# A fused FFN, delta-rule and FFN kernel on one core: where the second norm and the key pieces stand in the eight steps of a block

## What is computed

```
x = x + 0.5 * ffn(layernorm(x))      # recurrent over the batch index b = 0..7
x = x +       attn(layernorm(x))     # recurrent over the 1024 tokens
x = x + 0.5 * ffn(layernorm(x))

ffn, step b:  f = sigmoid(x_b Wf + c Uf + bf);  i = sigmoid(x_b Wi + c Ui + bi)
              g = tanh(x_b Wc + c Uc + bc);     c = f * c + i * g
     result:  tanh(x_b Wo + c_final Uo + bo)
attn:         s = x W^T;  k = rmsnorm of each head (16 heads of 16) of x
              per token, head: S = lam*S; S += beta * k (v - k^T S); o = k^T S, v = -s
              result: layernorm(s + o)
```

## Time and profile before

| | |
|---|---|
| median of three runs | 1555.78 us |
| profiled execution | 1562.62 us, its span 1560.8 us |
| TensorE matmul, weight load | busy 1380.0 us (88%), 1277.7 us (82%) |
| VectorE, ScalarE, GpSimd | 924.6 us (59%), 689.2 us (44%), 197.3 us (13%) |
| chain that ended last | TensorE 61%, VectorE 21%, issue 9%, ScalarE 7% |
| mean granted TensorE clock | 0.94 |
| period 4 (stage alone) | 96.5 us, TensorE busy 87.7 |
| period 8 (joined stage) | 145.5 us, TensorE busy 126.6 |
| period 12 (no pieces left) | 82.2 us, TensorE busy 78.6 |

### The profile page before, as it was taken

The page is one execution under the profiler, slowest core; times in us unless marked ns, Lnnn a source line. Parts: engine busy times, 40 slices in busy tenths (PEclk is TensorE's granted clock), DMA queues, the critical chain, the costliest instruction groups (busy, mean ns, idle before and its releaser), DMA issues.

```text
span 1560.8 us, 61982 instructions
## 1 busy us (share of the span) xinstructions
PE 1380.0 (88%) x27811; PEld 1277.7 (82%) x27811; DVE 924.6 (59%) x2208; ACT 689.2 (44%) x1585; POOL 197.3 (13%) x230
## 2 busy tenths in 40 slices
PE   4889899998989899888888988889899999999887
PEld 4878798888979788777877887878788989898776
DVE  2646686777867766558655774664444645554532
ACT  2253454545445444443444444344445445444332
POOL 0001010010100100002400320040130404040400
PEclk9999999998999989998889979989999999999999
DMA  4011112112211323232224222421534333332000
GB/s 128 1 41 68 42 44 84 58 75 67 78 63 58 124 64 95 91 119 65 73 82 131 68 90 64 158 70 47 166 88 119 98 110 107 90 122 80 28 28 28
DMA packets 64201, 125.39 MB, mean 80 GB/s; under 512 B 12352, under 2 KB 33088, under 8 KB 61888
## 3 DMA queue, kind: packets, MB, share of 16 engines
q1 hardware_dynamic: 63936, 121.43, 24.3%
HBM read 62.13 MB, written 59.24 MB: 78 GB/s over the span
## 4 chain that ended last, share of the span: by engine, by line
PE 61%; DVE 21%; issue 9%; ACT 7%; DVEq 0%; ACTq 0%
PE ps L426 29%; PE ps L493 7%; PE ps L1007 6%; PE ps L818 4%; PE ps L642 4%; PE ps L991 4%; DVE ln_bn L83 3%; ACT gates L443 3%; PE ps L667 2%; ACT ffn_rows L101 2%; DVE ig L469 2%; PE ps L386 1%; ACT gates L450 1%; PE ps L478 1%; DVE prod L743 1%
## 5 line engine op out<-in xcount | busy, mean ns | idle before, releaser
L426 PE MATMUL ps<-cst,wt 128*128 128x128 f32 x2688 | 360.7, 290 | 8.3 <-DVE cst L471 7.8
L426 PEld LDWEIGHTS ps<-cst,wt 128*128 128x128 f32 x2688 | 331.3, 201 | 20.0 <-DVE cst L471 9.1
L426 PE MATMUL ps<-ffn_rows,wt 128*128 128x128 f32 x2304 | 300.3, 288 | 17.4 <-DVE hs L506 6.4
L426 PEld LDWEIGHTS ps<-ffn_rows,wt 128*128 128x128 f32 x2304 | 285.7, 203 | 25.9 <-issue 15.8
L465 DVE TENSOR_TENSOR fc<-gates,cst 128x256 f32<-128x256 f32 x112 | 51.7, 461 | 285.0 <-ACT gates L443 284.9
L443 ACT ACTIVATE gates<-ps,colv 128x128 f32<-128x128 f32 x448 | 127.1, 365 | 173.9 <-PE ps L426 173.6
L1007 PE MATMUL ps<-e,kgb 32*128 32x64 f32 x4032 | 129.6, 275 | 7.9 <-issue 4.1
L1007 PEld LDWEIGHTS ps<-e,kgb 32*128 32x128 f32 x4032 | 120.6, 189 | 16.6 <-issue 10.6
L1096 POOL TENSOR_TENSOR ffn_rows<-ffn_rows,rowv 128x256 f32<-128x256 f32 x64 | 54.3, 882 | 573.5 <-DMA ffn_rows<-x_scratch 573.5
L818 PE MATMUL ps<-inv_cols,kv 32*32 32x32 f32 x8192 | 92.4, 201 | 34.3 <-DVE zbd L1037 17.4
L618 POOL TENSOR_TENSOR kg_rows<-key_rows,g_tok 128x512 f32<-128x512 f32 x32 | 46.4, 1478 | 594.9 <-DVE key_rows L581 594.9
(11 more groups left out here) (117 smaller groups left out, 1793.5 us busy)
## 6 DMA issues: line engine op xcount, KB each, us to landing
kg_scratch<-kg_rows SPq DMA_DIRECT2D x32, 512.0 KB, 3.9
xs_scratch<-xs_out SPq DMA_DIRECT2D x32, 512.0 KB, 3.6
xsb<-xs_scratch SPq DMA_DIRECT2D x64, 256.0 KB, 3.5
kgb<-kg_scratch SPq DMA_DIRECT2D x256, 64.0 KB, 2.6
ffn_rows<-x SPq DMA_DIRECT2D x32, 256.0 KB, 3.4
x_scratch<-ffn_rows SPq DMA_DIRECT2D x32, 256.0 KB, 2.7
e_scratch<-e SPq DMA_DIRECT2D x256, 32.0 KB, 1.7
ffn_rows<-e_scratch SPq DMA_DIRECT2D x8, 1024.0 KB, 6.2
```

Source lines behind the costliest of these rows:

```text
L426: mm = pe.matmul(banks[g][:, col:col + P], wt[:, w, k, m * P:(m + 1) * P], rhs, start=(x in (0, FI)), stop=(k == KT - 1 and (t == 0 or x > ...
```

## The change

The table `PERIOD` is rewritten, and two pieces are cut in two. ln2 keeps the statistics, and the coefficients become lc2. apply becomes apa and apb, four rows each. gt0 goes from the first list of step 1 to the second of step 0, ahead of the statistics. lc2 and apa stand in step 1 behind gt1; inv1 and apb in step 2's first list; lt0 in its second; lt1, v01, v23, tt0 and tt1 follow half a step later each than before, as do ta0 to ta2. ln1 goes from the end of step 5 to its first list, lc1 to the first of step 6, ap0 to the second of step 6 and ap1 to the first of step 7. The square waits for the whole apply by a semaphore, on the engine that does the apply itself.

```diff
-PERIOD = {0: ([(2, "g3")], [(1, "ln2")]),
-          1: ([(3, "ta4"), (2, "gt0")], [(2, "gt1"), (3, "ta5"), (2, "inv1"), (1, "apply")]),
-          2: ([(1, "lt0"), (3, "ta6")], [(1, "lt1"), (2, "al"), (1, "square"), (2, "inv2")]),
-          3: ([(3, "ta7"), (1, "v01")], [(1, "v23"), (2, "inv3"), (1, "sums")]),
-          4: ([(2, "tt0")], [(2, "tt1"), (1, "rms"), (1, "key")]),
-          5: ([(2, "ta0")], [(1, "keys"), (2, "ta1"), (-1, "ln1")]),
-          6: ([(1, "kt0"), (2, "ta2")], [(1, "kt1"), (1, "km0"), (-1, "lc1")]),
-          7: ([(1, "g0"), (-1, "ap0")], [(1, "g1"), (1, "km1"), (-1, "ap1")])}
+PERIOD = {0: ([(2, "g3")], [(2, "gt0"), (1, "ln2")]),
+          1: ([(3, "ta4")], [(2, "gt1"), (1, "lc2"), (3, "ta5"), (1, "apa")]),
+          2: ([(2, "inv1"), (3, "ta6"), (1, "apb")], [(1, "lt0"), (2, "al"), (1, "square"), (2, "inv2")]),
+          3: ([(1, "lt1"), (3, "ta7")], [(1, "v01"), (1, "sums"), (2, "inv3")]),
+          4: ([(1, "v23")], [(2, "tt0"), (1, "rms"), (1, "key")]),
+          5: ([(2, "tt1"), (-1, "ln1")], [(1, "keys"), (2, "ta0")]),
+          6: ([(1, "kt0"), (2, "ta1"), (-1, "lc1")], [(1, "kt1"), (2, "ta2"), (1, "km0"), (-1, "ap0")]),
+          7: ([(1, "g0"), (-1, "ap1")], [(1, "g1"), (1, "km1")])}
...
             if name == "ln2":
                 dve.wait_ge(ff.x_done, 4 * (n + 1))
                 ln2.stats_bn(dve, n, xt[b.p], bn_buf[0])
+            elif name == "lc2":
                 ln2.coefficients_bn(dve, n, bn_buf[0])
...
-            if name == "apply":
+            if name in ("apa", "apb"):
                 if n > 0:
                     filled(act, "gt", n - 1, 3)
-                ln2.apply(act, n, xn2, xt[b.p], range(8))
+                ln2.apply(act, n, xn2, xt[b.p], range(4) if name == "apa" else range(4, 8))
...
             elif name == "square":
+                act.wait_ge(ln2.applied, 8 * (n + 1))
                 act.activation(key_half, key_rows, ACT.Square).then_inc(sq_done, 1)
```

## The result

The changed kernel takes 1633.31 us (median of 4, 1629.45 to 1635.51), the kernel before on the same chip 1559.35 (4 runs, 1555.32 to 1564.24): ratio **1.047**, 95% interval 1.0426 to 1.0514. It is 74 us slower where 45 were forecast, and above the forecast's high end of 1625. A repeat beside other runs gave 1634.34 us, ratio 1.0504 (1.0452 to 1.0557).

A forecast was written before the change was run, and what follows sets the result against it. It took TensorE's queue to bound the kernel, lengthened by waits at its head and the half clock behind them. The alone stage's 31.9 us plus the joined stage's 13 made 45 us, so 1601 us, range 1557 to 1625.

The forecast's parts named there:

- alone stage: Periods 0 to 5, without the state hops: new costs 59.6 us against old 27.7 in periods 2 to 5, net +31.9.
- old gt wait: Step 1, periods 2 to 5: TensorE's wait for gt0's banks goes, 15.1 us, with 10.4 of half clock behind it.
- joined stage: Periods 6 to 9, where the state hops run beside the step: +3.6 us for each of 6 to 8, +13 together.
- term (c): Joined stage, step 3: inv1 now lies ahead of VectorE's z copy, for which TensorE stands: +3.6 us.
- Term (b): Joined stage: ScalarE's copy of e now stands behind half an apply that awaits gt1's eviction and the coefficients: +2.1 us on the hop.
- Term (a): Joined stage: gt0 waits for its Gram eviction: +0.5 us.
- term (d): Joined stage: v23 leaves step 3 and lt1 enters: -2.6 us.
- Step 4 gets v23 and loses one inverse copy: even: Joined stage, step 4: the values piece that enters and the copy that leaves cancel, so no cost.
- The port question: Step 5: L469 gets back 0.85 us beside GpSimd, sum unchanged; tt1's copy 1.6 us later only at the upper end.
- Faster: Rival: al in step 2 and ta0 do not wait, only the removed wait counts: -22 us, 1534; chance 0.13.
- No change: Rival: the waits come but the clock stays high and the joined stage absorbs its own: +11 us, 1567; chance 0.11.
- One wait only: Rival: al's bank is free in time, ta0's wait stays with its half clock: +17 us, 1572; chance 0.12.

The follow-up runs named there:

- e1: The new table in periods 0 to 5 alone, the old order from period 6 on: 1597.66 us, ratio 1.0264 to the kernel before.
- e4: The changed kernel with al put ahead of lt0 in step 2: 1635.34 us, ratio 1.0518 to the kernel before.
- e5: The changed kernel with tt0 and tt1 put back where they stood in step 4: 1606.90 us, ratio 1.0299 to the kernel before.
- e9: The kernel before, in periods 0 to 5 alone, with only gt0 moved to step 0 behind the third Gram part: 1543.27 us, ratio 0.9909.
- e6: The changed kernel with inv1 put back at the end of step 1: 1616.28 us, ratio 1.0384 to the kernel before.
- s3: The kernel before, from period 6 alone, with only inv1 moved from step 1 to the head of step 2: 1570.09 us, ratio 1.0076.
- s2: The kernel before, from period 6 alone, with the norm pieces, gt0, lt and the values moved as in the change: 1571.96 us, ratio 1.0097.
- e11: The changed kernel with the values v01 and v23 put back in step 3: 1640.65 us, ratio 1.0527 to the kernel before.
- s1: The kernel before, from period 6 alone, with the solve pieces tt0 to ta2 moved later as in the change: 1576.20 us, ratio 1.011.
- e10: The kernel before, in periods 0 to 5 alone, with only the norm's coefficients moved behind gt0 in step 1: 1543.38 us, ratio 0.9902.
- e3: The changed kernel with the unit ta1 moved back from step 6 to behind ta0 in step 5: 1633.65 us, ratio 1.0492 to the kernel before.

## Why the forecast was wrong, and where it was right

**The alone stage: right in its waits.** In period 4 gt0 waits 1.50 us (forecast 1.5), al 3.88 (4.5), ta0 4.10 (3.7); cst of step 5 comes 13.1 us after that of step 4 (14). Behind gt0 and al the X takes 4.47 us, behind ta0 4.57, not 5.5; the forecast had put slower matmuls behind two of these waits and none behind gt0. In period 2 al waits only 2.07 us, but lt0 ahead of it waits 3.66 for the apply, for which the forecast had no term. The sum was +31.9 against +32.3 in the profile, of which TensorE's idle made 24 (waits forecast: 21.5) and its busy time 9 (half clock forecast: 10.4); the repeat has +35.9, e1 +36.7. e4 and e5 confirm the queues by moving them. But the match is partly luck, two errors that cancel. I priced the old gt wait and its half clock at 25.5 us and the gt0 wait that replaces it at 6, a gain of 19.5. e9, which does only that, gained 13.6 in periods 1 to 5. So the removal was over-priced by 6. All the rest was forecast at 31.9 + 19.5 = 51.4 and measured 32.3 + 13.6 = 45.9, over-priced by about as much.

**inv1: right.** In the alone stage undoing it changed nothing beyond the scatter (e6); in the joined stage term (c), 3.6 us in each of three periods, 10.8 in all, is what s3 lengthened periods 6 to 9 by: 10.8. The wait and its size are right; that they agree to the tenth is luck, given a scatter of some 6 us between traces. TensorE's waits grew by more (14.8).

**The copy of e, al and lt: one sized right, one too low, two not priced.** Term (b), +2.1 per hop, was 6.3 for three; the hop's update waits 5.4 us longer in s2. Term (a), 1.5 for three, is gt's wait: 3.3 us where there was none. Not on the list were al, which waits for ScalarE in the joined stage too (+4.0), and lt (+3.0). And term (d), -2.6 for each of three periods, was work moved and counted as gain: in s2 the step without v23 got 10.8 us shorter over the four periods, and the step with it 10.3 longer. e11 says the same from the other side. Forecast for the part 0, measured +11.0, or +15 by its runs.

**The solve pieces: the step that failed.** The record says "Step 4 gets v23 and loses one inverse copy: even", and has no line at all for ta0, ta1 and ta2 in the joined stage. s1 measures this: +22.2 us in periods 6 to 9 of its profiled execution, +16 by the medians, either way the largest of the three parts and near half of the stage's loss. tt1's bank must wait for the z copy of the hop, which VectorE does behind the rms chain and the key product: 9.5 us in s1, and 5.9 more than gt and tt waited before; the changed kernel shows it in period 8:

```profile
968.73 2.29 DVE L582 TENSOR_TENSOR key_rows<-key_rows,rms 128x2048 f32<-128x2048 f32 x1
...
971.27 1.39 DVE L1039 COPY zbd<-ps 16x512 f32<-16x512 f32 x2
...
972.80 1.14 PE L804 MATMUL ps<-ident,inv 128*128 128x128 f32 x8 [3.71 <-DVE zbd L1039]
```

That is the rule of the code that `refill` waits in this stage for the state copies of the last hop. I had used it for ta in step 3 and not for the piece that newly stands first in a step. Another 6.6 is idle without a semaphore (the last section says what comes with it), and what is left, 9.7, is slower matmuls: TensorE's busy time in these periods rose by 9.6 us (477.4 to 487.0), and the half-clock length by 30.8 us, or 44 against the other kernels with the old order. The forecast priced half clock in the joined stage at zero, except for the upper end.

So 13 forecast was 10.8 (c), about 0 for the norm pieces and the solve pieces, +2 for period 9; measured apart by the traces, 10.8, 11.0 and 22.2. Two terms were at or near nothing without a reason that held: the solve pieces, and v23's move, a gain of 7.8 that did not exist. In the changed kernel the two late parts also meet, as lt1 waits 7.66 and 5.03 us in periods 7 and 8 for the z copy behind inv1, here in period 8 (12.7 in all; 4.1 in e6, 3.0 in s2, none in s3); in exchange ta waits less. Its total, 39.9, is below the sum of the parts, 44.0, by no more than the traces scatter.

```profile
935.04 1.39 DVE L1039 COPY zbd<-ps 16x512 f32<-16x512 f32 x2
...
936.58 1.94 PE L633 MATMUL ps<-ident,key_rows 128*128 128x128 f32 x8 [5.03 <-DVE zbd L1039]
```

**The port question.** The copy L756 from PSUM beside GpSimd's products took 1.98 us, no longer than elsewhere (2.04 at 426.74 in the same period), L469 took 0.42 us where it had 1.28, and GpSimd's four products 4.10 where they had 6.57. L469 says nothing by itself here, since it starts at 439.02 and GpSimd had ended at 438.60; but in e5, where it again stands beside GpSimd's products, it took 1.27. The upper end's term of 1.6 us a period did not come. This is as the Trainium skill has it ("SBUF — State Buffer", Who interferes with whom): a VectorE operation with two inputs in SBUF contends with a GpSimd operation that reads SBUF, one with at most one such input, outside the two-port modes, does not. The change of place was worth about 0.85 us on a product behind another wait, and did not show in the time.

**The rivals.** Faster (1534) fell with al's wait of 3.88 us; its gain was real but belonged to one edit: e9 and e10 have it at 1543, without the pieces that follow. The Trainium skill ("Perfetto Trace Analysis", Optimizing Scalar/DVE Operations) says that breaking up instructions may let work end sooner where ScalarE or VectorE cause bubbles elsewhere. No run here splits a single instruction, so none tests this by the letter. For groups of instructions both outcomes are on record: e10, where the coefficients were cut off and put behind an eviction, gained 1%; the change put the cut apply and the eviction of ta6 ahead of the gates in ScalarE's queue, and al's wait went from 0.55 to 3.88 us. No change (1567) supposed a high clock; it was 0.92 over the span, after 0.94. One wait only (1572) fell as both waits came.

**Still open.** How much of the half clock belongs to which idle stretch, and what in s1 brings the clock down from step 6 to 7 of three periods and not of period 8: no run keeps the clock and leaves the waits. Nor does a run try the change without its solve pieces in the joined stage alone.

## What to carry to other kernels

A piece that is cut out of a full queue paid where it was put behind the one eviction that TensorE waits for; each further piece that is then moved must be checked at its new place for what now stands ahead of it on every engine, and for the gate of that place (here a state copy), not for the work that it takes along. Work moved from one step to another is no gain: e3, e11 and s2 each gave one step what they took from its neighbour. And idle stretches of 1 to 4 us are to be priced with the slower matmuls behind them: by the traces of periods 1 to 9 the change added some 54 us of idle to TensorE and 18 us to its busy time with the same matmuls.

## What the runs showed of the hardware

Runs of small matmuls have idle stretches that no semaphore explains, most of them of 0.3 to 3 us. They sum to 26 to 36 us over periods 6 to 9 in every kernel, and in the repeat most of them stand at the same places (L820 1.02 and 0.92 us, L993 1.71 and 1.99, from step 6 to 7 of period 6). Moving ta1 moved them with it: in e3 they fell from 10.1 to 4.4 us in one step and rose from 3.0 to 9.0 in the step before.

The DMA records of the traces show what comes with them. The page of the changed kernel has this queue:

```profile
q8 instruction: 219, 3.59, 0.9%
```

These are 219 packets of 16384 bytes. TensorE has 27811 matmuls and as many weight loads; if the queue is TensorE's, that is 64.5 bytes an instruction and some 254 instructions a packet (an estimate from these numbers), about one unit of 128 matmuls with their weight loads. In the changed kernel 39 idle stretches over 0.4 us are named "issue". Seven stand ahead of ta0 and one ahead of gt, where the code waits. The other 31 all end 1.2 to 1.6 us after such a packet has landed (in the kernel before 1.2 to 1.75); of the 71 waits over 0.4 us that a semaphore explains, 7 do. In the kernel before it is 32 of 36 (the other four stand ahead of tt), in s1 33 of 36 (ta0). In the rows of s1 above TensorE goes on at 1079.87 and 1083.77, and the packets landed at 1078.49 and 1082.39. So these stretches look like waits for instructions: a unit of 128 small matmuls uses up a packet in 1.29 us, and here the next one landed 3.9 us after the last. It is shown by the times alone; no run changed how the instructions arrive.

The clock of s1's step 6 to 7 shows how little an idle stretch alone tells. In period 9 the clock fell to 1.2 GHz at 1079.5, for 10.2 us, during an idle of 1.06 us in the second unit (1078.81 to 1079.87). In period 8 an idle of 1.07 us at the same place was followed by 2.4 GHz. Ahead of the first the clock had been back at 2.4 GHz for 3.5 us, ahead of the second for some 10. What decides between the two, no run shows.
